# The cross-attention stage of a decoder layer: score rounds, copies, cuts and the top-32 search in a new order

## The reference, cut to what matters

```python
scores = jnp.einsum('bthd,bghd->bhtg', Q, K) / np.sqrt(DH).astype(np.float32)
scores = jnp.where(vision_mask[:, None, None, :], scores, -jnp.inf)
topv, topi = jax.lax.top_k(scores, K_TOP)
probs = jax.nn.softmax(topv, axis=-1)
attn = jnp.zeros_like(scores).at[bi, hi, ti, topi].set(probs)
attn_mean = attn.mean(axis=1)
c_t = jnp.einsum('btg,bgd->btd', attn_mean, V)
scale_in, shift_in = jnp.split(c_t @ W_film_in + b_film_in, 2, axis=-1)
x = x * (1.0 + mod_gate * scale_in) + mod_gate * shift_in
y = s4d(x, log_dt, A_re, A_im, C_re, C_im, D_skip)
```

## Time and profile before

| | us |
|---|---|
| median of 3 runs (4732.20 to 4735.45) | 4734.09 |
| the profiled execution, its own time | 4733.47 |
| its span, first to last instruction | 4731.5 |
| TensorE busy | 4137.0 |
| VectorE busy | 3682.2 |
| ScalarE busy | 2066.3 |
| GpSimd busy | 2286.5 |

### The profile page before, as it was taken

The page is one execution under the profiler, slowest core; times in us unless marked ns, Lnnn a source line. Parts: engine busy times, 40 slices in busy tenths (PEclk is TensorE's granted clock), DMA queues, the critical chain, the costliest instruction groups (busy, mean ns, idle before and its releaser), DMA issues. The chain is left out here.

```text
span 4731.5 us, 71840 instructions
## 1 busy us (share of the span) xinstructions
PE 4137.0 (87%) x28037; PEld 3050.4 (64%) x28066; DVE 3682.2 (78%) x5121; ACT 2066.3 (44%) x3816; POOL 2286.5 (48%) x2260
## 2 busy tenths in 40 slices
PE   8999995669999999999999999974799898998984
PEld 6777772347776677677667767773566666666652
DVE  5666667789999999999999999852567776776767
ACT  3343331145555444544444454411345454454543
POOL 1111114726665578887888778811333333333320
PEclk9999997769999888888888889987999999999997
DMA  2111115231112011111112111234411111111101
GB/s 89 48 46 52 48 43 192 52 109 37 36 37 74 19 34 41 48 56 34 41 39 65 34 41 34 61 94 176 125 53 57 52 50 48 54 50 59 46 22 38
DMA packets 214597, 276.08 MB, mean 58 GB/s; under 512 B 96659, under 2 KB 144403, under 8 KB 210224
## 3 DMA queue, kind: packets, MB, share of 16 engines
q1 hardware_dynamic: 196850, 216.91, 15.2%
q0 software_dynamic: 17408, 54.56, 3.3%
HBM read 186.44 MB, written 84.98 MB: 57 GB/s over the span
## 5 line engine op out<-in xcount | busy, mean ns | idle before, releaser
L1608 POOL TENSOR_TENSOR c_s<-c_s,c_z 128x2048 f32<-128x2048 f32 x128 | 583.6, 4559 | 520.1 <-ACT c_z L1378 520.0
L1932 PE MATMUL f_p_g<-f_hT,f_w 128*128 128x128 f32 x4096 | 539.0, 295 | 68.3 <-ACT f_gT L2032 53.9
L1932 PEld LDWEIGHTS f_p_g<-f_hT,f_w 128*128 128x128 f32 x4096 | 527.4, 211 | 88.9 <-ACT f_gT L2032 56.7
L1188 PE MATMUL c_p_a<-c_diag,c_s 128*128 128x128 f32 x4096 | 535.5, 295 | 31.6 <-ACT c_diag L1392 31.5
L1188 PEld LDWEIGHTS c_p_a<-c_diag,c_s 128*128 128x128 f32 x4096 | 528.4, 212 | 47.3 <-ACT c_diag L1392 36.8
L1368 ACT ACTIVATE c_s<-c_p_s 128x512 f32<-128x512 f32 x512 | 277.2, 594 | 544.8 <-PE c_p_s L1179 544.4
L1940 PE MATMUL f_p_o<-f_w,f_gT 128*128 128x512 f32 x1024 | 481.8, 592 | 0.0
L1240 PEld LDWEIGHTS c_p_m<-c_aT,c_vals 128*128 128x128 f32 x3072 | 412.3, 220 | 77.1 <-issue 73.4
L1240 PE MATMUL c_p_m<-c_aT,c_vals 128*128 128x128 f32 x3072 | 429.8, 307 | 2.4 <-ACT c_aT L1397 2.1
L1259 PE MATMUL c_p_m<-c_wf,c_uT 128*128 128x512 f32 x768 | 365.5, 613 | 6.7 <-ACT c_fi L1407 5.2
L1178 PE MATMUL c_p_s<-c_kt,c_qT 32*128 32x512 f32 x1024 | 328.5, 705 | 15.0 <-ACT c_s L1368 12.3
(11 more groups left out here) (370 smaller groups left out, 8707.0 us busy)
## 6 DMA issues: line engine op xcount, KB each, us to landing
mod_out<-c_fo POOLq DMA_DIRECT2D x32, 512.0 KB, 5.1
f_mr<-mod_out SPq DMA_DIRECT2D x32, 512.0 KB, 5.1
p_ct<-in_ctxT SPq DMA_DIRECT2D x16, 768.0 KB, 5.0
c_vals<-in_ctx SPq DMA_DIRECT2D x4, 3072.0 KB, 11.7
c_kb<-kspec SPq DMA_DIRECT2D x22, 512.0 KB, 3.6
a_xt<-in_xT SPq DMA_DIRECT2D x32, 256.0 KB, 3.1
a_xr<-in_x SPq DMA_DIRECT2D x32, 256.0 KB, 2.6
x<-a_out POOLq DMA_DIRECT2D x32, 256.0 KB, 2.5
```

The source lines that it names most:

```text
L1188: last = mm(p_a[:, n, :], s[:, j % RING, n * P:(n + 1) * P], diag[:, j % 2, :], start=(h == 0 and n % 4 == 0), stop=(h == NH2 - 1 and n % ...
L1608: pool.tensor_tensor(row, row, low, ALU.subtract).then_inc(cut_ready, 1)
L1932: last = mm(p_g[:, f % 8, :], w1[:, k, f * P:(f + 1) * P], hT[:, k * P:(k + 1) * P], start=(k == 0 and f % 4 == 0), stop=(k == KD - 1 and ...
```

## The change

- The score rounds stand otherwise among TensorE's work: a round of the second pair leads the tile, `attn(j+1)` closes it, `spectra` comes behind the fourth round, and `slot` behind `attn(j)`.
- ScalarE and GpSimd have new orders. On GpSimd `transform` comes ahead of `cut(j+1)`, `convolved` is split into `product` (ahead of `cut(j+2)`) and `half_way` (behind it), and `store_mod` comes later. On ScalarE `weigh(j+1)` comes behind `below(j+2)`, and three copies change places. `copy_s` waits for each half of a pair by itself.
- On VectorE the first part of a head's search in `lower` (the fold and three passes) is done among the last passes of the head before. The 16 found in `lower` are written beside `upper`, so that the passes over `upper` run over 1,040 elements and give the exact 32 largest; the threshold is the last of them, and the two instructions at L1550 and L1551 are gone.
- The keys and the mask's row are loaded in quarters, each behind the last score round that reads the old one.

```diff
+        HK = N2 // 2
+        upper, lower, low = z[:, 16:HK + 16], z[:, HK + 32:N2 + 32], z[:, N2 + 32:]
+        seconds = [z[:, 0:16], z[:, HK + 16:HK + 32]]
+        listed = [z[:, 0:HK + 16], z[:, 16:HK + 32]]
...
-            def load_keys(b):
-                at_least(sp, s_done, b * CH * 16)
-                sp.dma_start(kt[:], keysT[:, b * N2:(b + 1) * N2]).then_inc(keys_in, 16)
+            def load_keys(b, c):
+                at_least(sp, s_done, (b * CH - 1) * 16 + 8 + 2 * c + 2 if b else 0)
+                cols = slice(c * 512, (c + 1) * 512)
+                sp.dma_start(kt[:, cols], keysT[:, b * N2 + c * 512:b * N2 + (c + 1) * 512]).then_inc(keys_in[c], 16)
                 for h in range(NH2):
-                    sp.dma_start(mrow[HS * h:HS * h + 1, :], mask_row[b:b + 1, :]).then_inc(keys_in, 16)
+                    sp.dma_start(mrow[HS * h:HS * h + 1, cols], mask_row[b:b + 1, cols]).then_inc(keys_in[c], 16)
```

TensorE's tile, `more` being t + 1 < TILES:

```diff
+                scores(t, 1, 0)
                 if t:
                     attn(j - 2)
-                scores(t, 1, 0)
+                scores(t, 1, 1)
                 if t > 1:
                     film(t - 2, 1)
-                scores(t, 1, 1)
-                if t + 1 < TILES:
+                scores(t, 1, 2)
+                if more:
                     turn(t + 1)
-
                 if t:
                     attn(j - 1)
-                scores(t, 1, 2)
-                if t + 1 < TILES:
+                if more:
                     queries(t + 1)
+                scores(t, 1, 3)
                 if forward_job(t) is not None:
                     spectra(t)
-                scores(t, 1, 3)
+
+                if more:
+                    scores(t + 1, 0, 0)
                 if t:
                     context(t - 1, 0)
-
                 attn(j)
-                if t + 1 < TILES:
-                    scores(t + 1, 0, 0)
+                if slot_job(t) is not None:
+                    slot(t)
+                if more:
+                    scores(t + 1, 0, 1)
                 if t:
                     context(t - 1, 1)
-                if t + 1 < TILES:
-                    scores(t + 1, 0, 1)
+                if more:
+                    scores(t + 1, 0, 2)
                 if t:
                     context(t - 1, 2)
-
-                attn(j + 1)
-                if t + 1 < TILES:
-                    scores(t + 1, 0, 2)
-                if slot_job(t) is not None:
-                    slot(t)
-                if t + 1 < TILES:
+                if more:
                     scores(t + 1, 0, 3)
                 if t:
                     film(t - 1, 0)
+                attn(j + 1)
```

ScalarE:

```diff
             def copy_s(t, p, c):
-                at_least(act, attn_done, (t - 1) * NH2 + 2 * p + 1)
                 for i in range(2):
+                    at_least(act, attn_done, (t - 1) * NH2 + 2 * p + i)
...
-                a(tb[:, par:par + 1], thr[:, par:par + 1], ACT.Copy, scale=STEEP).then_inc(tb_ready, 1)
+                a(tb[:, par:par + 1], top[:, par, 31:32], ACT.Copy, scale=STEEP).then_inc(tb_ready, 1)
+                at_least(act, w_ready, j - 1)
...
                     diagonal(j - 1)
+                copy_s(t, 1, 1)
                 if t > 1:
                     copy_fo(t - 2)
-                copy_s(t, 1, 1)
-                if t + 1 < TILES:
+                copy_s(t, 1, 2)
+
+                below(j)
+                if more:
                     copy_x(t + 1)
-
-                below(j)
                 if t:
                     copy_a(t - 1)
-                copy_s(t, 1, 2)
-                if t + 1 < TILES:
+                if more:
                     copy_q(t + 1)
+                copy_s(t, 1, 3)
                 weigh(j)
                 diagonal(j)
                 if forward_job(t) is not None:
                     copy_f(t)
-                copy_s(t, 1, 3)
 
                 below(j + 1)
-                if t + 1 < TILES:
+                if more:
                     copy_s(t + 1, 0, 0)
-                if t + 1 < TILES:
                     copy_s(t + 1, 0, 1)
-                weigh(j + 1)
+                if slot_job(t) is not None:
+                    copy_slot(t)
                 diagonal(j + 1)
+                if more:
+                    copy_s(t + 1, 0, 2)
+
+                below(j + 2)
                 if t:
                     copy_u(t - 1)
-
-                below(j + 2)
-                if t + 1 < TILES:
-                    copy_s(t + 1, 0, 2)
-                if slot_job(t) is not None:
-                    copy_slot(t)
-                if t + 1 < TILES:
+                if more:
                     copy_s(t + 1, 0, 3)
-                else:
+                weigh(j + 1)
+                if not more:
                     copy_fi(TILES - 2)
                 weigh(j + 2)
                 diagonal(j + 2)
```

VectorE's head:

```diff
-                dve.wait_ge(s_copied, (j // 2 + 1) * 8)
-                at_least(dve, sum_done, j - 1)
-                st.mark(v.tensor_tensor(upper, row[:, 0:N2 // 2], row[:, N2 // 2:], ALU.max))
-                st.behind(v.tensor_tensor(lower, row[:, 0:N2 // 2], row[:, N2 // 2:], ALU.min))
-                st.behind(v.max(best[0], upper))
-                st.behind(v.max(other[0], lower))
-                st.behind(v.match_replace(upper, best[0], upper, NEG))
-                st.behind(v.match_replace(lower, other[0], lower, NEG))
-                st.behind(v.max(best[1], upper))
-                st.behind(v.max(other[1], lower))
+                at_least(dve, z_done, j)
+                st.link(fold(j, upper, ALU.max))
+                at_least(dve, sum_done, j - 1)
+                st.link(v.max(best[0], row))
+                st.link(v.match_replace(row, best[0], row, NEG))
+                st.link(v.max(best[1], row))
+                st.behind(v.match_replace(row, best[1], row, NEG))
                 if j:
                     invert(j - 1)
-                for n in range(1, 3):
-                    st.link(v.match_replace(upper, best[n], upper, NEG))
-                    st.link(v.max(best[n + 1], upper))
-                late = top[:, par, 16:32]
-                st.link(v.tensor_tensor(late, late, second[:, ::-1], ALU.max))
-                v.tensor_reduce(thr[:, par:par + 1], top[:, par, 15:32], AX.X, ALU.min).then_inc(z_done, 1)
                 if j < LAST:
-                    dve.wait_ge(z_done, j + 1)
+                    st.behind(fold(j + 1, lower, ALU.min))
+                    st.behind(v.max(best[2], row))
+                    st.behind(v.max(nxt[0], lower))
+                    st.behind(v.match_replace(row, best[2], row, NEG))
+                    st.behind(v.match_replace(lower, nxt[0], lower, NEG))
+                    v.max(best[3], row).then_inc(z_done, 1)
+                    st.wait()
+                    st.mark(v.max(nxt[1], lower))
```

GpSimd's tile:

```diff
-                masked_identity(t)
                 j = t * NH2
                 if t:
                     cut(j - 1)
                 if t > 1:
                     modulate(t - 2)
-                    store_mod(t - 2)
+                masked_identity(t)
                 cut(j)
-                if ready and not of_kernel(ready):
+                if begun and not of_kernel(begun):
                     finished(t - 1)
-                cut(j + 1)
                 if job is not None:
                     transform(t)
+                cut(j + 1)
+                if inverse:
+                    product(t)
+                if t > 1:
+                    store_mod(t - 2)
                 cut(j + 2)
-                if job is not None and not of_kernel(job):
-                    convolved(t)
+                if inverse:
+                    half_way(t)
```

More of the change, by code:

```diff
@@ L923, in cross @@
         tb = m.sb("tb", [P, 2])
-        thr = m.sb("thr", [P, 2])
-        second = m.sb("second", [P, 16])
         den = m.sb("den", [P, 2])
@@ L944, in cross @@
         yb = m.sb("yb", [P, RX, CB])
-        upper, lower, low = z[:, 0, 0:N2 // 2], z[:, 0, N2 // 2:], z[:, 1, :]
-        other = [second[:, 8 * n:8 * n + 8] for n in range(2)]
-        fb_raw = z[:, 0, :][0:BR, :]
-        fb_part = z[:, 1, :].bitcast(BF16)[0:BR, 0:4 * D]
+        HK = N2 // 2
+        upper, lower, low = z[:, 16:HK + 16], z[:, HK + 32:N2 + 32], z[:, N2 + 32:]
+        seconds = [z[:, 0:16], z[:, HK + 16:HK + 32]]
+        listed = [z[:, 0:HK + 16], z[:, 16:HK + 32]]
+        fb_raw = z[0:BR, 32:N2 + 32]
+        fb_part = low.bitcast(BF16)[0:BR, 0:4 * D]
         kd = kb[:].rearrange("p a b c -> p (a b c)")[0:CB, :]
@@ L963, in cross @@
         rv = planes(kt[:])
-        rk = [planes(z[:, u, :]) for u in range(2)]
+        rk = [planes(z[:, 32:N2 + 32]), planes(low)]
         row_a, row_b, row_c = (cx[:].rearrange("p a n c -> p (a n c)"), mrow[:].bitcast(F32),
@@ L985, in cross @@
                 "ri_copied").split()]
+        keys_in = [m.sem(f"keys_in{c}") for c in range(4)]
         cx_in = [m.sem(f"cx_in{u}") for u in range(2)]
```

(15 more changed lines are left out.)

27 lines of the change are left out of this document (19 added, 8 removed).

## The result

The changed kernel takes 4658.26 us (median of 4 runs, 4653.16 to 4659.99), the kernel before 4734.77 on the same chip: a ratio of 0.9837, 95% interval 0.982 to 0.9854, so 1.6% faster. The profiled execution of the changed kernel took 4659.99 us beside its span of 4658.0.

What follows compares the result with a forecast made beforehand. VectorE was taken to bound the first stretch and a ring through GpSimd and ScalarE the second. There 52.9 + 3.3 + 7.9 + 1.0 gave 65.1 us a tile, 63 us off 4733.5: 4670 us, range 4590 to 4732.

Steps and rivals of the forecast that it cites:

- VectorE's head: VectorE's search of one head: 14.80 us falls to 14.51, so 58.0 us a tile instead of 59.2.
- The ring: Second stretch, GpSimd from cut(j) to the next tile's cut(j), including a wait for ScalarE: 64.1 us a tile.
- the piece over ScalarE: From the end of cut(j-1), ScalarE's weigh through below(j), while GpSimd waits: 7.9 us of the tile.
- the gap ahead of attn(j-2): TensorE still waits there about 3 us a tile for cut, weigh and diagonal of head j-2.
- The clock term: TensorE's low clock behind its remaining gap, delaying film and copy_fo: 1.0 us a tile added, between nothing and 2.2.
- second stretch: Twenty tiles, heads 45 to 125, with inverse transforms running: 68.26 us a tile falls to 65.1, 63 us off.
- Folds against GpSimd: VectorE folds meeting two-input GpSimd instructions: seven meetings a tile instead of four, 3 more at 1.1, 3.3 us.
- rival (3): VectorE's lower folds wait behind whole cuts, up to 4.5 us each: slower, 4778 us; chance 0.12.
- First stretch: First ten tiles, heads 0 to 40, 59.96 us each: change taken as 0, bounds -1.2 and +1.5 us a tile.
- Rival (1): VectorE becomes the bound in both stretches, 62.4 us a tile where inverse transforms run: 4603 us; chance 0.24.
- Rivals (2): TensorE's slow clock keeps the tile at 68.3 us where inverse transforms run: 4715 to 4735 us; chance 0.17.
- (4): The wait only moves and the ring closes elsewhere at 68 us a tile: 4725 to 4742 us; chance 0.05.

Runs made afterwards that it cites:

- e3: Changed kernel with one GpSimd multiplication done twice at the head of product: 4718.24 us, ratio 0.9975 to the kernel before.
- e4: Changed kernel with the first GpSimd multiplication of modulate done three times: 4663.99 us, ratio 0.9859 to the kernel before.
- e7: Changed kernel with VectorE's first pass over the next head's lower half reading 8 elements in place of 1,024: 4632.61 us.
- e9: Changed kernel with three repeats of a score matmul filling TensorE's gap ahead of attn(j-2), from tile 12 on: 4661.53 us.
- e6: Changed kernel with four repeats of a score matmul ahead of attn(j-2) in every tile: 4710.27 us.
- e8: Changed kernel with the keys and the mask's row loaded whole again, not in quarters: 4655.61 us.
- e11: Changed kernel with GpSimd's half_way split, four of its eight instructions moved behind cut(j+3): 4660.41 us.
- e12: Changed kernel with half_way split likewise and ScalarE's third score copy moved behind below(j) and copy_x, the attention copy later too: 4615.93 us.

## Why the prediction was right, and where its sizes were off

*VectorE's head.* 14.51 us in the sum; the heads that meet nothing step 14.50. z_done 1.14 us before the head's end is what the trace shows, too.

*The ring.* The mechanism stands, by e3 (2.8 us a tile for one more multiply), e4 (nothing in the slack) and e7 (nothing for 4 us less VectorE work a tile). Its parts: GpSimd without a wait 52.9 + 3.3 = 56.2 in the sum, 55.4 in the trace; the piece over ScalarE 7.9 + 1.0 = 8.9, and 9.27 in the trace. 65.1 against 64.8 us. The idle time ahead of cut(j) was to be about 4 us and is 4.3; the gap ahead of attn(j-2) about 3 and is 3.0; VectorE's 4.7 us wait is gone. On average over the 19 tiles it is 55.4 + 9.4 = 64.8: 0.8 us too much in the sum for GpSimd and 0.5 too little behind it cancel in part.

*The clock term.* This step is wrong as put, and that the sum is right in spite of it is luck. I added 1.0 us because copy_fo waits for film behind the low clock. It does wait (27.1 us in 19 times, 1.4 each), and attn(j-2) takes 5.46 us at the low clock against 3.74. The 7.9 us for ScalarE's piece at full clock was right: in e9's tiles at 1.00 ScalarE is ready at 5.45 us, and 2.3 us more to cut(j) make 7.8. But the tile did not get shorter there, so the low clock is worth 0.2 us a tile, not 1.0. What I had missed is the second way, 9.26 us over the fold that stands behind cut(j+3) and VectorE's passes; it is 1.4 us longer than the 7.9 of my piece, and the 1.0 stood in its place.

The page "TensorE: Matmul & The Clock Gate" of the Trainium skill, section "Loop structure matters more than you think", holds that the loop nest decides whether matmuls stay warm. The trace agrees in part: the granted clock in the second stretch rose from 0.88 to 0.96, with the gap ahead of turn() gone. (1 - 0.96) x 64.8 = 2.6 us a tile are still lost, of 8.2 before. One gap stayed and with it the low clock behind it, as the row had it, and the tile went by the ring.

*Folds against GpSimd.* I counted three more meetings at 1.1 us and took the wait behind a whole cut for unlikely. In 1671 to 2930 us 38 of 156 folds take over 3 us, two a tile: the upper fold beside half_way and the lower one behind cut(j+3). So rival (3) was partly there, with its mechanism and one of its waits a tile. It didn't decide, since the point from which it would wasn't reached: all that the folds take above 1.2 us is 131 us, 6.8 a tile, where 10.3 were needed. VectorE's own account closes too, 58.0 + 6.8 = 64.8 us, as it must for an engine that is hardly ever idle; e7 is what shows that it does not set the tile. By the Trainium skill, page "SBUF — State Buffer", section "Who interferes with whom", whoever issues first keeps the pair for its whole instruction. The traces now agree for waits of 2.6 us (3.80 against 1.20) and, in e7, of 4.3 us behind a whole cut (5.50 against 1.20). They do not agree everywhere: in the last section a fold begins first and is served last, and there the measurement decides.

*First stretch.* The mis-sized term. I set -1.2 for VectorE's gain against +1.5 for late scores or a late cut and took 0; it was -0.7 a tile (59.96 to 59.3; most tiles 59.0), 7 us in all. Scores are there in time, by 0.9 us (e6), and two heads of four pay 0.5 us for a fold that meets a GpSimd instruction. The forecast's 63 us off are 73.5 in the profiled execution: 6.4 more from the second stretch, 6.8 from the first, 2.7 from the tile between them and 3.9 from the last three heads and what follows, less 9.4 at the beginning of the stage.

*The stage's beginning.* Its first load is issued at 953.0 us before and at 960.3 after, though all code ahead of it is unchanged; over all fourteen profiled executions it lies anywhere from 953.0 to 961.0, the kernel before having the earliest. I take 7 of the 9.4 us for that scatter; that is argued, not shown. The rest is mostly the first head's lower half, searched ahead of the loop: from the first fold to the last pass of head 0 it takes 17.1 us in place of 14.5. Quarters or whole keys make no difference (e8).

*Rival (1)* would have been read as true from a single number, VectorE 99% busy. The tile of 64.8 against 62, and e7, speak against it. *Rivals (2) and (4)*: the tile is neither 68.3 nor is the clock at 0.88.

What stays open: which of the moves in the orders pays; what VectorE's way would let through if its fold did not meet cut(j+3); and the cause of the late first load.

## What to carry to other kernels

A search or a pass that is moved forward to use a gap moves its input's due time forward as well: alone it cost 160 us here, and with the producers' orders changed first it gave about 30. Before a slack is filled, look for a second way of the same length between the same two events; here VectorE's way shortened alone (e7), ScalarE's alone (e9 at full clock) and GpSimd's alone (e11) gave nothing in the second stretch, and shortening all of them (e12) gave about 40 us. And an engine that is 99% busy may be waiting inside its instructions: take work from it and see whether the time moves.

## What the hardware showed that was not expected

A VectorE fold can stand behind two GpSimd instructions, not only one. In the timeline of the changed kernel above, the fold of 2480.45 begins while L862 runs (until 2481.39), L863 begins at 2481.34 and ends at 2482.60 at its usual 1.26 us, and only then does the fold do its 1.1 us, until 2483.70; the instruction after that, L864, takes 1.33 us in place of the 0.46 of its equals. It is so in all 19 tiles (the fold takes 3.2 to 3.3 us there). The fold began 0.9 us before L863 and yet came behind it. It is not so everywhere: the fold of 2488.92 is served as soon as the cut ends, ahead of L1638, which takes 2.26 us in place of its 1.27. What decides which of the two happens, these runs don't show.

And the clock can be at 0.53 behind TensorE work without a gap (e6, 2652 us), where the same work 131 us earlier had 1.00; what decides it these runs don't show either.
